# Attention with strips of two steps in one group, a third probability buffer, one projection matmul per slot, and the high part made on VectorE

## The reference

```
q, k, v = x @ wq.T + bq, x @ wk.T + bk, x @ wv.T + bv      # split into 16 heads of 32
scores  = einsum('bhqd,bhkd->bhqk', q, k) / sqrt(32)
ctx     = einsum('bhqk,bhkd->bhqd', softmax(scores), v)
x       = layernorm(x + ctx @ wo.T + bo)
```

## Time and profile before

| | |
|---|---|
| median of 3 runs | 2248.66 us (2243.45 to 2250.18) |
| profiled execution | 2244.02 us, span 2242.3 us |
| TensorE busy | 2136.4 us, 95% |
| VectorE busy | 1238.4 us, 55% |
| GpSimd busy | 891.7 us, 40% |
| ScalarE busy | 851.4 us, 38% |
| granted TensorE clock, mean | 0.987 |

### The profile page before, as it was taken

How to read it: one execution, slowest core, us unless ns; L and a number is a source line. 1 busy time by engine, 2 the same in 40 slices (tenths; PEclk the granted TensorE clock), 3 DMA queues, 4 the chain that set the end, 5 groups by cost and what they waited for, 6 DMA issues and landing times. The chain is left out here.

```text
span 2242.3 us, 34860 instructions
## 1 busy us (share of the span) xinstructions
PE 2136.4 (95%) x9654; PEld 1188.3 (53%) x9655; DVE 1238.4 (55%) x2242; ACT 851.4 (38%) x1508; POOL 891.7 (40%) x861
## 2 busy tenths in 40 slices
PE   7999999999999999999999998789999999999997
PEld 5555445554444544445554432368744444446886
DVE  6767666476667366666467761458222222224875
ACT  2255554255555245555255564221111111111332
POOL 2254754344755344764445455510111111112651
PEclk9999999999999999999999999899999999999999
DMA  4221433203431402421403301572222222223762
GB/s 141 67 62 31 100 72 77 101 17 66 105 77 38 134 21 62 105 56 47 137 25 70 74 11 46 196 264 101 80 90 85 92 86 91 88 90 122 228 189 72
DMA packets 94515, 202.74 MB, mean 90 GB/s; under 512 B 24576, under 2 KB 25088, under 8 KB 92416
## 3 DMA queue, kind: packets, MB, share of 16 engines
q1 hardware_dynamic: 83456, 164.96, 25.3%
q0 software_dynamic: 10880, 35.66, 5.9%
HBM read 110.65 MB, written 39.06 MB: 67 GB/s over the span
## 5 line engine op out<-in xcount | busy, mean ns | idle before, releaser
L765 DVE TENSOR_REDUCE max_half<-ps_side 128x1 f32<-128x512 f32 x1024 | 663.3, 683 | 333.4 <-PE ps_side L532 323.6
L683 ACT ACTIVATE probs<-ps_s 128x512 f32<-128x512 f32 x1024 | 573.5, 596 | 487.2 <-PE ps_s L549 399.3
L469 POOL TENSOR_TENSOR acc<-probs 128x512 f32<-128x512 f32 x384 | 484.7, 1289 | 487.4 <-ACT probs L683 481.1
L549 PE MATMUL ps_s<-kq_stack 97*128 97x512 f32 x1024 | 461.4, 454 | 23.4 <-ACT probs L683 14.3
L532 PE MATMUL ps_side<-kq_stack 96*128 96x512 f32 x1024 | 399.6, 401 | 10.9 <-DVE max_half L765 7.2
L549 PEld LDWEIGHTS ps_s<-kq_stack 97*128 97x128 f32 x1024 | 192.5, 189 | 361.1 <-ACT probs L683 224.1
L560 PE MATMUL ps_ctx<-probs,v_sb 128*32 128x512 f32 x2048 | 274.4, 608 | 0.0
L1429 PE MATMUL ps_gu<-gu_sb,xT_e 128*128 x576 | 261.3, 596 | 0.5 <-issue 0.3
L1327 POOL DMA_INDIRECT x_g<-x,who_all x72 | 68.3, 948 | 458.4 <-PE ps_t L1419 357.7
L532 PEld LDWEIGHTS ps_side<-kq_stack 96*128 96x128 f32 x1024 | 195.9, 191 | 44.9 <-DVE max_half L765 13.8
L1550 ACT ACTIVATE act_g<-ps_gu 128x256 f32<-128x256 f32 x72 | 27.6, 383 | 351.3 <-PE ps_gu L1429 351.3
(11 more groups left out here) (199 smaller groups left out, 2512.5 us busy)
## 6 DMA issues: line engine op xcount, KB each, us to landing
kq_stack<-kq SPq DMA_DIRECT2D x192, 256.0 KB, 5.0
y_slots<-y_t SPq DMA_DIRECT2D x72, 256.0 KB, 2.3
res<-inv_rows SPq DMA_DIRECT2D x128, 64.0 KB, 2.0
probs<-x SPq DMA_DIRECT2D x16, 512.0 KB, 5.2
x_r<-x SPq DMA_DIRECT2D x32, 256.0 KB, 3.4
x_t<-x SPq DMA_DIRECT2D x32, 256.0 KB
gu_sb<-wgu SPq DMA_DIRECT2D x8, 1024.0 KB, 16.2
out<-gu_sb SPq DMA_DIRECT2D x32, 256.0 KB, 2.6
```

The source lines that it names most:

```text
L469: nc.gpsimd.tensor_tensor(acc[:, h, :], probs[:, (loc - 1) % 2, h, :] if j == 1 else acc[:, h, :], probs[:, loc % 2, h, :], ALU.add).then_ ...
L549: nc.tensor.matmul(ps_s[:, (loc * HG + h) % RING, :], k_stack[par][0:3 * HD + 1, h, kt * P:(kt + 1) * P], q_stack[par][0:3 * HD + 1, h, ha ...
L683: nc.scalar.activation(probs[:, loc % 2, h, :], ps_s[:, (loc * HG + h) % RING, :], ACT.Exp, scale=HD ** -0.5).then_inc(probs_ready, 1)
L765: nc.vector.reduce_max(max_half[:, u // 2, u % 2:u % 2 + 1], bank, AX.X).then_inc(side_free, 1)
```

## The change

1. `weighted` of both steps of a pair runs behind the second one, with `row_sums` right behind: twelve strips in a row. For that `probs` gets a third buffer: step `loc` uses buffer `loc % 3`. The outer two stay, the middle one, `probs_mid`, lies over `wv_lo`. So `wv_lo` is stored to DRAM in the prologue and loaded back (1 MB) ahead of each tail, behind the last use of the middle buffer and ahead of the last `spread` in SyncE's queue; TensorE waits for it (`wv_moved`).
2. `exps` wait for the sums of the pair that used their buffer, not for folds. At a batch's start they wait for the tail's reads of x, and for x2's stores only in the middle buffer.
3. A projection unit is twelve single matmuls, at slot offsets 0, 1, 2, 3, 4, 4, 5 to 10 from slots 1, 15, 29 and 43. The low part stays two slots behind the last one.
4. `high` moves from ScalarE (at the unit's last matmul) to VectorE (right ahead of `low`), but for the prologue.
5. The tail's banks are rotated by three.

```diff
-PROJ_FROM, PROJ_EVERY, PROJ_UNIT = 2, 3, 14
+PROJ_FROM, PROJ_UNIT = 1, 14
+PROJ_SLOTS = (0, 1, 2, 3, 4, 4, 5, 6, 7, 8, 9, 10)
+UNIT = 3 * C
+PROBS = 3
...
-        for i in range(PROJ * C):
-            slot = PROJ_FROM + PROJ_UNIT * (i // C) + PROJ_EVERY * (i % C)
+        for i in range(PROJ * UNIT):
+            slot = PROJ_FROM + PROJ_UNIT * (i // UNIT) + PROJ_SLOTS[i % UNIT]
             plan[slot].append(("proj", i))
-            if i % C == C - 1:
-                plan[slot + LOW_LATER].append(("low", i // C))
+            if i % UNIT == UNIT - 1:
+                plan[slot + LOW_LATER].append(("low", i // UNIT))
...
+        with nc.sbuf_tensor("probs_mid", [P, HG, HALF], F32) as probs_mid:
+            pass
         wv_lo = sb("wv_lo", [P, C, D], F32R)
...
-        probs = sb("probs", [P, 2, HG, HALF])
+        probs_outer = sb("probs_outer", [P, 2, HG, HALF])
+        def probs(loc, h):
+            return probs_mid[:, h, :] if loc % PROBS == 1 else probs_outer[:, loc % PROBS // 2, h, :]
...
+        def tail_bank(i):
+            return ps_side[:, (i + SIDE_RING) % TAIL_RING, :]
...
+                if not last and g == G - 1:
+                    sp.wait_ge(pv_done, (b + 1) * BSTEPS - FOLD)
+                    sp.wait_ge(sum_done, (b + 1) * SUMS - 1)
+                    sp.sem_inc(passed_sp, 1)
+                    sp.dma_start(wv_lo[:].bitcast(F32), wv_lo_kept).then_inc(wv_moved, 16)
...
             spread(0, 0)
+            sp.wait_ge(wv_split, C)
+            sp.dma_start(wv_lo_kept, wv_lo[:].bitcast(F32)).then_inc(wv_moved, 16)
...
-                    if g == 2 and i < NHALF:
-                        pe.wait_ge(x_split, (b + 1) * CHUNKS + i * C + c + 1)
-                    piece(n, i, c, ps_proj)
+                    if g == 2 and i < NHALF and r % 3 == 0:
+                        pe.wait_ge(x_split, (b + 1) * CHUNKS + i * C + r // 3 + 1)
+                    product(i, r, ps_proj)
...
-                        if slot == SLOTS - 1:
-                            weighted(b, loc)
-                            if loc % FOLD == FOLD - 1:
-                                row_sums(b, loc)
+                        if slot == SLOTS - 1 and loc % FOLD == FOLD - 1:
+                            for done in range(loc - FOLD + 1, loc + 1):
+                                weighted(b, done)
+                            row_sums(b, loc)
...
                 pe.wait_ge(side_free, base_of(b * G + G))
+                pe.wait_ge(wv_moved, 16 * (b + 2))
...
-                if loc >= 2:
-                    act.wait_ge(pv_done, b * BSTEPS + loc - 1)
-                    if h < FOLD_POOL:
-                        act.wait_ge(folded, (b * FOLDS + folds(loc - 2) - 1) * FOLD_POOL + h + 1)
-                    else:
-                        act.wait_ge(folded_dve, (b * FOLDS + folds(loc - 2) - 1) * FOLD_DVE + h - FOLD_POOL + 1)
-                else:
-                    if h == 0:
-                        act.wait_ge(tail_free, b * TAIL + KT // 2 * (loc + 1))
-                    if loc == 0:
-                        act.wait_ge(x2_out[h + 2], 16 * (b + 1))
-                nc.scalar.activation(probs[:, loc % 2, h, :], ps_s[:, (loc * HG + h) % RING, :],
+                if loc >= PROBS:
+                    act.wait_ge(pv_done, b * BSTEPS + loc - PROBS + 1)
+                    act.wait_ge(sum_done, b * SUMS + (loc - PROBS) // FOLD + 1)
+                elif loc == 0:
+                    act.wait_ge(tail_free, b * TAIL + (KT if isinstance(b, int) and b == 0 else h + 1))
+                elif loc == 1:
+                    if isinstance(b, int) and b == 0:
+                        act.wait_ge(wv_moved, 16)
+                    act.wait_ge(x2_out[h + 2], 16 * (b + 1))
+                elif h == 0:
+                    act.wait_ge(tail_free, b * TAIL + KT)
+                nc.scalar.activation(probs(loc, h), ps_s[:, (loc * HG + h) % RING, :],
...
         @block.vector
         def _(dve):
+            def high(n, u, bank, g):
+                sel, half = u // 2, slice(u % 2 * HALF, (u % 2 + 1) * HALF)
+                dve.wait_ge(proj_ready, PROJ * n + u + 1)
+                for s in stacked:
+                    dve.wait_ge(s, SPREAD * n)
+                nc.vector.tensor_scalar(kq[:, HI[sel], half], bank, bkq[:, sel, g:g + 1], None,
+                                        ALU.add).then_inc(proj_hi, 1)
...
                 if kind == "low":
+                    if not (isinstance(m, int) and m < 0):
+                        high(m + 2, u, ps_proj, (g + 2) % G)
                     low(m + 2, u, ps_proj, (g + 2) % G)
```

More of the change, by code:

```diff
@@ L185, in attention @@
         wo_in = sem("wo_in")
+        wv_moved = sem("wv_moved")
         few_in = sem("few_in")
@@ L500, in three, with product @@
                 return done
[L502 to L509 removed]
+            def product(u, r, bank):
+                sel, half, c = u // 2, u % 2, r // 3
+                w = (wkq_hi, wkq_lo, wkq_hi)[r % 3][:, sel, c, :]
+                xs = (x_hi, x_hi, x_lo)[r % 3][:, c, half * HALF:(half + 1) * HALF]
+                done = nc.tensor.matmul(bank, w, xs, start=r == 0, stop=r == UNIT - 1)
+                if r == UNIT - 1:
                     done.then_inc(proj_ready, 1)
@@ L616, in _ @@
                     pe.wait_ge(x_split, u % 2 * C + c + 1)
-                    piece(0, u, c, ps_side[:, u % 2, :])
+                    for k in range(3):
+                        product(u, 3 * c + k, ps_side[:, u % 2, :])
             pe.wait_ge(wv_split, C)
```

46 lines of the change are left out of this document (20 added, 26 removed).

## The result

The changed kernel takes 2284.97 us (median of four runs, 2278.53 to 2290.36) against 2246.05 us (2242.44 to 2250.18) for the kernel before on the same chip: a ratio of 1.0174, 95% interval 1.0158 to 1.0191. It is slower by 39 us, outside the range. The profiled execution took 2280.1 us with a span of 2278.4; the mean granted clock of TensorE is 0.973, before 0.987. Two of the four runs took 2279 and 2280 us at a mean clock of 0.973, two 2290 us at 0.966 and 0.968; the profile is of one of the shorter.

A forecast was written before the change was run, and what follows sets the result against it. TensorE, busy 95% of the span, was taken as the bound. Terms -74 + 55 + 17 + 8 - 3 - 2 = +1 us on the profiled 2244.0, 4.7 under the median, gave 2249 us; range 2216 to 2271 (8 in 10).

The forecast's parts named there:

- part 2: One projection per slot: 2.8 of a group's 4.9 us of TensorE waits, nearly all for ScalarE's exponentials, go.
- Part 5: Load and store of V's low weights: load delays the tail's stacks, +8 us (bounds 0 and 15); prologue store costs nothing.
- Part 6: Batch starts no longer wait for x2's stores, -3 us; last batch's third group, -2; its fourth, nothing.
- the prediction's three signs of being wrong: Gate under 0.5 us, first strip joins costing more than 0.88, or the batch's tail growing by over 5 us.
- Parts 1 and 2: Strips in one group (2.4 us a group) and one projection per slot (2.8): -74 us over fourteen groups.
- Part 3: High part on VectorE: next projection unit waits for the low part (the gate), 3.9 us a group, +55 us.
- Part 4: x's chunks in third groups: TensorE waits for GpSimd's splits, +5.5 in three batches, +17 us; bounds 0 and 27.
- The cheap gate: Rival: projections' wait for the low part costs half (2222 us, chance 0.30 for about half) or nothing (2194, 0.08).
- The slow one, GpSimd's chain: Rival: third groups' folds and splits cost their upper bound and set later pairs, +10 to +20, 2259 to 2269; chance 0.17.
- ScalarE as the bound in every slot: Rival: exponentials bound every slot, not bare ones only, so spreading's 39 us stay, 2288 us; chance 0.08.

The follow-up runs named there:

- experiment 7: Experiment 5 with each step's weighted sums behind its own step again (strips apart), third buffer kept: 2228.08 us, 0.9928 of the kernel before.
- experiment 5: Changed kernel with high part on ScalarE; in third groups first unit at old slots in threes, units ordered K0, Q0, K1, Q1: 2211.41 us, 0.9863 of before.
- experiment 6: Experiment 5 with the high part on VectorE, so the changed kernel with only the chunks mended: 2252.71 us, 1.0029 of the kernel before.
- experiment 3: Changed kernel with projections at the old slots in threes and high part on ScalarE; grouped strips and third buffer stay: 2249.74 us, 1.0028 of before.
- experiment 8: Experiment 5 with the low part one slot sooner (LOW_LATER = 1): 2204.85 us, 0.9829 of the kernel before.
- experiment 11: Experiment 9 with second to fourth projection units starting at slots 16, 30 and 44 and packed closer: 2209.49 us, 0.9828 of the kernel before.
- experiment 9: Experiment 8 with each step's strips apart in the last group of the last batch alone: 2201.97 us, 0.9801 of the kernel before.

## Why the prediction was wrong, step by step

Experiments 7, 5 and 6 and the two kernels form a chain: before 2244.3; projections spread and chunks mended, with the third buffer, the load of V's weights and the new waits of `exps` 2228.1 (-16.3); strips grouped 2211.4 (-16.7); high part on VectorE 2252.7 (+41.3); chunks as in the change 2283.3 (+30.6). The links add up to +39 by construction. The last three add one thing each, the first one bundles part 2 with parts 5 and 6. A link's size also hangs on what stands beside it: on the old projections and unmended chunks (experiment 3) grouping with all that goes with it won nothing. None of the prediction's three signs of being wrong came: the gate was over 0.5, the joins 0.88, the chain in the tail no longer.

- **Parts 1 and 2, -74: the step that failed most.** The runs give -33, parts 5 and 6 included. The join of strips was right (0.88, pairs 0.32 to 0.36 shorter), but I multiplied it by eight pairs without asking what the lone strips had covered. Experiment 7 shows that: they gave ScalarE time for a bank (10.9 us of waits become 21.4, in slots 8 to 15 and 24 to 31), and grouped they cost 4.2 in the last group. A group gains 1.5, not 2.4. Spreading gains 1.2 in a batch's first group (72.2 to 71.0) and 1.4 in others, not 2.8. With the moved multiplications counted (0.235 each), slots 16 to 23 gain 0.68, 32 to 39 and 48 to 55 0.34, 24 to 31 and 0 to 7 about 0.2, slots 8 to 15 and 56 to 63 nothing, and slots 40 to 47 lose 0.38. That loss is a wait for the low part of 0.40, 14 times in experiment 7, where I had none without the high part ahead of it; experiment 8 takes it away. I took the 4.9 us of a group that were not multiplication as ScalarE's waits, removable but for three bare runs, and had no row for that: the view of that group (160.6 to 232.7 us) shows TensorE idle for 1.3 us in all ahead of scores, 0.5 of it ended by ScalarE, and how the rest divides no view shows. My sums were also 0.4 a group too good: three bare runs at 0.24 + 0.1 make 1.0 and not 0.8, and slots 56 to 63 by their own figures 1.5 and not 1.3. That is 6 of the 74.
- **Part 3, +55: the mechanism right, the size somewhat high.** 39 waits of 1.06 us on the mean (0.78, 1.15 and about 1.18 by slot), where I had 0.97, 1.2 and 1.45. The high part took 0.73, near my upper bound; VectorE did start operations 0.60 apart. But the gate takes the place of other waits: with it those for ScalarE are 7.9 us and without it 21.8, and 5.6 us of waiting for the low part are there without it too. So a group grows by only 2.3 (69.4 to 71.7, table), 32 us in fourteen. Of the other 9, four pairs with a fall of the clock in experiment 6 are 6; the rest stays open.
- **Part 4, +17: the waits were right, the clock behind them was missing.** The three waits came within 0.2 us (3.05 for 3.2, 3.35 for 3.4, and 1.60 for 0.97 of gate with 0.7 more). But slots 0 to 23 of third groups stand 12.9, 14.0 and 13.9 above ordinary ones (27.0), where I had 8.9; before, 3.3 to 3.6 above. That is +30 in three batches, 13 us over the term (8.9 less 3.6 is 5.3 a batch, which I wrote as 5.5). The trace divides it. TensorE's idle time over an ordinary group's is 8.0, 8.0 and 7.7 us there. The granted clock over these 40 to 41 us is 0.87, 0.83 and 0.83 (1.00 before), so 10, 14 and 14 us ran at 1.2 GHz, one to two of them inside the waits. Half of the rest is some 4.6 to 6 us. The two add up to 12.6, 13.9 and 13.7: an estimate from these windows and waits, and it leaves nothing over.
- **The clock was in no step.** By the mean clock of the two profiles, time at 1.2 GHz rose from 58 to 123 us; as TensorE is the bound, these 65 us can have cost up to half of that, 32 of the 39 us. By what runs of one kernel show (25 us more at 1.2 GHz, 12 us more time, experiment 3) it is some 30. They are not a further term but lie inside the chunks', the gate's and the last group's. A pair that holds such a stretch takes 1.4 to 1.9 us longer than its like. In the changed kernel the falls come inside or within 1.5 us behind single waits of 2.6 to 3.9 us and of 1.55 at a batch's end, behind some gates of 1.1 but not behind most, and in the last group among waits of 0.2 to 0.5. The kernel before has such a stretch at the end of its tail (0.87 in the window from 430 to 440 us), so it could have been asked for. The changed kernel's extra falls lie at the chunks, in the fourth groups, at the end of a batch, at one gate of the last batch and in the last group.
- **Part 5, +8: nothing in the tail.** The load did delay the stacks' landing, but not what I made depend on it: the chain from the first stack to the reciprocal became 1.1 us shorter, and my lower bound held. From the last row sums of a batch to the first of the next it is 64.4 and 64.6 us, before 65.8 twice, but with half as much time at 1.2 GHz; profiles of the experiments with as much of it as before have 66.0 to 66.4. The third is 60.1 in both. So parts 5 and 6 together cost some 0.6 a batch at most in the changed kernel, where +5 in all was forecast. The store in the prologue was put at nothing: the first row sums come at 98.5 us, before at 97.1, and at 97.7 to 100.2 in the experiments. No run is without the store alone, so its share is open.
- **Part 6, -3 and -2:** the first does not show beside part 5; the third group of the last batch takes 60.8 us (61.0 before), not 2 less; its fourth, said to be unchanged, takes 4.2 more.
- **The rivals.** The cheap gate is refuted by the 41.3 us. The slow one, GpSimd's chain, was priced at +10 to +20 over the forecast and is right as to its place; its rule, that the fold starts only after the pair's exponential, is seen at 260.14 (2.28 idle, ended by ScalarE). Part 4 came out 13 over its term, inside that price, but by the clock and not by GpSimd setting four pairs: from slot 24 on third groups are ordinary. That the price fits is luck. ScalarE as the bound in every slot is wrong: with spread projections and the gate its waits are 7.9 us, 27 times.
- **Sum by the runs:** -33 + 41 + 31 = +39, against -74 + 55 + 17 + 8 - 5 = +1. The -33 holds parts 5 and 6, so it stands against -71. The gains were counted at over twice their worth; the two costs together were right (72 and 72), but by errors of both signs, which is luck.

**Left open.** What makes the granted clock fall at one gate and not at another of the same length was not tried by itself; that the clock is the rest of part 4 is worked out from the trace's windows and waits, not from a run that changes it alone. No run leaves out the third buffer or the load and store of V's weights by itself, nor spreads the projections alone. Why packed units with the high part on ScalarE (experiment 11) end no better than experiment 9 is told by the pairs' lengths only.

## What to carry to other kernels

Before work is taken out from between two points of the bounding engine, ask who used that time: here ScalarE did, for the scores' banks, and more than half of the gain went back. A wait of the bounding engine is to be priced with the clock that follows it; where a group of equal pairs has one that is 1.5 to 2 us longer, look at the granted clock in a narrow window first. When an operation is moved to an engine that must be in time for a gate, move the gate by a slot in the same edit: that was worth 28 of 41 us here.

## What was not expected of the hardware

- TensorE's granted clock fell from 2.4 to 1.2 GHz inside or right behind single waits in otherwise dense work (0.66 in the window 262 to 272 us, from inside a wait of 3.35), and in the last group, where bare scores wait 0.2 to 0.45 us each in a row (0.94 over 53 us). Of the 6.8 us at half speed 5.8 lie behind that wait; half of them, 2.9 us, is nearly as much again as the wait itself.
- A 1 MB load issued ahead of twelve stack transfers in the same queue made them land 6.4 us after their issue in the median instead of 5.0, the first one 6.5 instead of 3.3. It did not lengthen the chain behind them: 24.2 us from the first stack's issue to the reciprocal, 25.35 without it.
- VectorE's tensor_scalar on 128x512 from PSUM took 0.73 us, ScalarE's same operation 0.69. VectorE started the next independent operation 0.60 behind one that lasts 0.67, and a dependent one 0.76 behind one of 0.73.
